# Values' three split terms as two stacked products and four bands, in the wide attentions of a four-layer transformer kernel

## The chip, the cores and the metric

The kernel runs on one core of one Trainium2 chip. The metric is the device time of a whole launch in microseconds: the median of the runs. The core has five engines with queues of their own that meet only through semaphores: TensorE (PE; its weight loads are the rows PEld), VectorE (DVE), ScalarE (ACT), GpSimd (POOL) and SyncE (SP), which here issues all transfers.

## The reference, cut to what matters

`x` is 128 x 64 tokens of width 128; `ctx_768`, the context, is 128 x 64 tokens of width 96. Four layers follow one another; each adds to `x` a cross attention of normalised `x` to the context and then a feed-forward part. All is float32.

```python
# layer: heads, width of a head      L0: 8, 128   L1: 16, 8   L2: 16, 64   L3: 16, 64
x = x + xattn(layernorm(x), ctx_768, Wq, Wk, Wv, Wo, bo)   # softmax over the 64 context tokens of a sequence
x = x + ffn(layernorm(x), ...)
```

L0, L2 and L3 are the "wide" attentions that the change touches; L1 is the "narrow" one. With M = Wv Wo of a head (96 x 128), the kernel forms a head's values as context times M, so that no output projection is left.

## The kernel before, in words

**Tiles.** The 8192 tokens are 64 tiles of 128, handled in 16 groups of 4 tiles (`NG`, `G`). `wide_attention` takes 4 heads per step: Q = 2 steps per group in L0 (`paired` is false, 32 steps), Q = 4 in L2 and L3 (`paired`, 64 steps each). That is 160 steps.

**Split products.** These matmuls take operands in a rounded format (`F32R`). For float32 accuracy each factor is split into a rounded high part and the rest, and `product` (L285 to L291) adds three matmuls of 512 columns: high x high (L288), low x high (L290), high x low (L291). For values the stationary side is 128 context tokens of `ct_hi` or `ct_lo` (96 rows) and the moving side `M_hi` or `M_lo` for 4 heads (96 x 512). So a step has 4 values products (V0 to V3, one per tile), 12 matmuls with 96 of the array's 128 rows used.

**A step on TensorE** (`group` on `block.tensor`): projections P0 and P1 (L288 to L291), transposes of the probabilities of the step two back (L577), P2, P3, V0, V1, V2, V3, then `output` (L598, 64 small matmuls for the step two back) and `scores` (L617, in L0 L620, 64 small ones). In the last step of a group the next group's tokens are transposed too (L237). P, T and V fills take turns in four PSUM banks (`Rotation`): V0 and V1 take the banks of the transposes, V2 and V3 those of P2 and P3, the next step's P0 and P1 those of V0 and V1. So V3 waits until ScalarE has kept P3 (`P_kept`), and P0 of the next step until V0 was copied out.

**The others in a step.** ScalarE, in this order: keep P0, P1 (L708), T0 (L718), exponentials of the step before (L723), T1, P2, P3, then values V0 and V2 (L713). VectorE: maxima and subtraction of the scores of the step before (L810, L813), extra work at fixed steps (normalising the next group, L220, at k = Q-2; `finish`, L837 and L305 to L313, at k = 2, in L0 at k = 0; in L0 the `quantise` steps of the first groups), totals and reciprocal (L818, L821), values V1 and V3 (L825), and at the group's end the split of the tokens (L254, L256). GpSimd: multiplication of the probabilities by the reciprocals (L511), and at k = 1 of each group from the second on `split_context` for the next group: high part (L389), then, behind a semaphore, the rest (L392). TensorE waits for it (`ct_split`) before P0 of the next group's first step.

**Start of a wide attention.** TensorE forms M for all heads (L541; in L0 also the folded query-key matrices, L539). ScalarE rounds it (`keep_folded`, L690), VectorE takes the rest (`keep_rest`, L786): 2 rounds in L0, 4 in L2 and L3. In L2 and L3 VectorE then does the token scales, for which ScalarE takes a square root (`scales.root`, L330) ahead of its first copy of P0; in L0 TensorE waits for all rests before it transposes the first tokens (L237).

**SyncE** loads the context of group j (96 x 512 floats, L377, L383) once the scores of group j-2 are done.

Of the kernel before, what the change touches and what calls it, by code (L numbers as in the profile page):

```python
# [14 lines left out]
F32 = mybir.dt.float32  # L15
# [392 lines left out]
def wide_attention(c, tag, heads, dh, scale):  # L408
# [3 lines left out]

    nc, dram = c.nc, c.dram
# [3 lines left out]
    with ExitStack() as st:  # L417
# [4 lines left out]
        M_hi, M_lo = (sb(f"M{n}{tag}", [K, heads, D], F32R) for n in ("_hi", "_lo"))  # L422
# [18 lines left out]
        fold_bank = (c.bank[1], c.bank[2], c.bank[3], c.bank[7]) if paired else (c.bank[1], c.bank[3])  # L441
# [3 lines left out]
        folded, hi_kept, lo_kept = sem("folded"), sem("hi_kept"), sem("lo_kept")  # L445
# [29 lines left out]
        with nc.Block() as block:  # L475
            @block.sync
            def _(sp):
# [10 lines left out]
                first_contexts(sp, c, "ctxP", ct, ct_in)  # L488
# [10 lines left out]
                later_contexts(sp, c, "ctxP", ct, ct_in, S_done, Q, 0)  # L499

            @block.gpsimd
            def _(pool):
# [3 lines left out]
                for j in range(2):  # L506
                    split_context(nc, pool, c, ct, ct_hi, ct_lo, j, j, 0, ct_in, ct_split)
# [6 lines left out]
                def group(i, slot, turn=None):  # L514
                    for k in range(Q):
                        if k or started(i, 1):
                            multiply(i * Q + k - 1, (slot * Q + k - 1) % 2)
                        if k == 1 and turn is not None:
                            split_context(nc, pool, c, ct, ct_hi, ct_lo, i + 1, 1 - slot, turn, ct_in, ct_split)
# [9 lines left out]
            def _(pe):  # L529
# [16 lines left out]
                else:  # L546
                    pe.wait_ge(lo_kept, 2 * rounds)
# [3 lines left out]
                def projection(m, i, slot, k, u, step):  # L551
                    x_parts = c.xT_hi[slot][:, :], c.xT_lo[slot][:, :]
                    ct_parts = ct_hi[slot][:, :], ct_lo[slot][:, :]
# [11 lines left out]
                def value(m, slot, k, u, step):  # L565

                    tok = slice(u * P, (u + 1) * P)
# [38 lines left out]
                def scores(m, i, slot, k):  # L606
                    for p in range(2):
                        for t in range(4):
                            for b in range(2):
                                for h in range(2):  # L610
# [8 lines left out]
                                    else:  # L619
                                        last = nc.tensor.matmul(out, proj[:, 2 * h + p, tok], ct[slot][:, ctx],  # L620
# [3 lines left out]
                def group(i, slot):  # L624
                    for k in range(Q):
# [24 lines left out]
                        if m == 0 and paired:  # L650
                            pe.wait_ge(lo_kept, 6)
# [14 lines left out]
                for n in (NS - 2, NS - 1):  # L666
# [9 lines left out]
                    output(n, n // Q, n % Q, n % 4)  # L676
# [3 lines left out]
            def _(act):  # L680
# [3 lines left out]
                def keep_folded(r):  # L684
# [5 lines left out]
                    nc.scalar.activation(M_hi[:, hs, :], fold_bank[r][0:K, :].rearrange("p (h d) -> p h d", h=4),  # L690
# [20 lines left out]
                def keep_value(m, u, step):  # L711
                    act.wait_ge(V_done, 4 * m + u + 1)
                    nc.scalar.activation(values[:, step % 4, u, :, :].rearrange("p h d -> p (h d)"),  # L713
# [47 lines left out]
            def _(dve):  # L761
# [37 lines left out]
                if paired:  # L799
                    keep_rest(2)  # L800
                    keep_rest(3)
# [21 lines left out]
                def keep_value(m, u, step):  # L823
                    dve.wait_ge(V_done, 4 * m + u + 1)
                    nc.vector.tensor_copy(values[:, step % 4, u, :, :].rearrange("p h d -> p (h d)"),  # L825
# [1753 lines left out]
```

## Time and profile before

| | us |
|---|---|
| median of 3 runs | 3574.77 (3566.44 to 3576.28) |
| profiled execution, its own time | 3565.56 |
| its span, first to last instruction | 3563.7 |
| TensorE, VectorE, ScalarE, GpSimd busy | 3440.1, 2463.3, 2024.0, 1244.5 |
| mean granted TensorE clock | 0.986 of full speed |

The profiled execution is 9.2 us below the median. Wide attentions lie at 0 to 394 us (L0), 1437 to 2071 (L2) and 2329 to 2963 (L3). In the timeline a row stands at its start, with its duration behind it; matmul durations overlap, so that their rate is read from the distance of the starts. "x2" means two in a row merged. What stands in brackets is the idle time of the engine before the row and who ended it.

### The profile page before, as it was taken

Reading aid. Unit: us, or ns where it says so; the run is one execution under the profiler, and the core shown is the slowest. Engines: PE = TensorE matmul, PEld = TensorE weight load, DVE = VectorE, ACT = ScalarE, POOL = GpSimd, SP = SyncE. Lnnn points to the kernel's source line nnn. Section 1 sums busy time; section 2 is a strip of 40 time slices with the busy share of each in tenths; the row PEclk is TensorE's granted clock in tenths of the full one; section 3 lists DMA queues with packets and bytes.
Section 4 is the critical chain, followed back from the end, with each engine's and each line's share of the span. In section 5 each row is a group of like instructions: output and inputs, shape, how many; then the busy total and the mean of one; then the engine's idle time right before and its main releaser. Section 6 shows DMA issues by size and latency. Waiting matters only on the chain. (4 is left out here: it accounts for less than half of the span.)

```text
span 3563.7 us, 99704 instructions
## 1 busy us (share of the span) xinstructions
PE 3440.1 (97%) x43493; PEld 2809.3 (79%) x43493; DVE 2463.3 (69%) x4927; ACT 2024.0 (57%) x3446; POOL 1244.5 (35%) x924
## 2 busy tenths in 40 slices
PE   7999999999999899999999999999999998999999
PEld 6887788887888555788888877778888886777777
DVE  8977555555666799666666656766666666777776
ACT  4445555554666787555555544455555555656564
POOL 1322233334554233222222223322222224555555
PEclk9999999999999899999999999999999999999999
DMA  3000000001000000000000000010000000000000
GB/s 110 11 11 11 1 1 1 1 1 38 15 15 9 1 1 1 18 9 7 7 9 7 5 22 1 1 47 9 7 7 9 7 5 1 7 7 13 7 7 13
DMA packets 15324, 40.66 MB, mean 11 GB/s; under 512 B 3083, under 2 KB 4683, under 8 KB 13994
## 3 DMA queue, kind: packets, MB, share of 16 engines
q1 hardware_dynamic: 14890, 34.28, 3.1%
q8 instruction: 345, 5.65, 0.7%
q14 instruction: 89, 0.73, 0.1%
HBM read 30.08 MB, written 4.19 MB: 10 GB/s over the span
## 5 line engine op out<-in xcount | busy, mean ns | idle before, releaser
L708 ACT ACTIVATE projL<-bank 128x512 f32<-128x512 f32 (+1 forms) x640 | 371.2, 601 | 647.3 <-PE bank L291 632.0
L511 POOL TENSOR_TENSOR probL<-probL,invL 128x1024 f32<-128x1024 f32 x160 | 304.7, 1904 | 1198.9 <-DVE invL L821 1198.9
L1704 POOL TENSOR_TENSOR h_loM<-hM,h_hiM 126x512 fp32r<-126x512 f32 x224 | 290.3, 1296 | 255.0 <-ACT h_hiM L1830 252.3
L598 PEld LDWEIGHTS bank<-valuesL,probTL 64*64 64x64 f32 x10240 | 277.7, 133 | 61.1 <-issue 55.2
L810 DVE TENSOR_REDUCE neg_maxL<-bank 128x16 f32<-128x1024 f32 x160 | 195.9, 1224 | 184.3 <-PE bank L617 153.4
L598 PE MATMUL bank<-valuesL,probTL 64*64 64x128 f32 x10240 | 316.4, 272 | 4.4 <-ACT probTL L718 4.4
L1403 PEld LDWEIGHTS bank<-w2T,hM 128*128 128x128 f32 x2304 | 278.4, 193 | 38.3 <-ACT hM L1458 22.9
L1403 PE MATMUL bank<-w2T,hM 128*128 128x128 f32 x2304 | 284.9, 277 | 15.4 <-ACT hM L1458 15.4
L1458 ACT ACTIVATE hM<-bank,ahead_scales 128x512 f32<-128x512 f32 x288 | 183.8, 684 | 189.3 <-PE bank L291 189.1
L825 DVE COPY valuesL<-bank 128x512 f32<-128x512 f32 x320 | 213.1, 679 | 109.5 <-PE bank L291 104.0
L818 DVE TENSOR_REDUCE totalL<-probL 128x16 f32<-128x1024 f32 x160 | 194.7, 1217 | 122.4 <-ACT probL L723 122.1
L1381 POOL TENSOR_TENSOR accM<-accM,partM 128x512 f32<-128x512 f32 x128 | 165.0, 1289 | 295.4 <-DVE partM L1488 295.4
L1942 DVE TENSOR_TENSOR tM<-bank,siluM 126x512 f32<-126x512 f32 x224 | 154.1, 688 | 115.9 <-PE bank L291 65.0
L713 ACT ACTIVATE valuesL<-bank 128x512 f32<-128x512 f32 x320 | 195.3, 611 | 56.4 <-PE bank L291 55.8
L1830 ACT ACTIVATE h_hiM<-hM 126x512 fp32r<-126x512 f32 x224 | 140.6, 628 | 133.1 <-DVE hM L1966 132.1
L718 ACT ACTIVATE probTL<-bank 128x512 f32<-128x512 f32 x320 | 188.3, 591 | 25.0 <-PE bank L577 25.0
L813 DVE TENSOR_TENSOR probL<-bank,neg_maxL 128x1024 f32<-128x1024 f32 x160 | 195.9, 1224 | 5.5
L1824 ACT ACTIVATE siluM<-bank 126x512 f32<-126x512 f32 x224 | 132.0, 590 | 97.1 <-PE bank L291 95.3
L1488 DVE TENSOR_TENSOR partM<-bank,gatesM 128x512 f32<-128x512 f32 x128 | 88.4, 690 | 128.4 <-PE bank L1403 127.2
L723 ACT ACTIVATE probL<-probL 128x1024 f32<-128x1024 f32 x160 | 169.3, 1058 | 2.9 <-DVE probL L813 2.8
L577 PEld LDWEIGHTS bank<-ident,probL 128*128 128x128 f32 x1280 | 149.9, 141 | 24.0 <-POOL probL L511 1.8
L577 PE MATMUL bank<-ident,probL 128*128 128x128 f32 x1280 | 167.2, 273 | 0.5 <-POOL probL L511 0.4
(300 smaller groups left out, 9033.3 us busy)
## 6 DMA issues: line engine op xcount, KB each, us to landing
ct0L<-in_ctxP SPq DMA_DIRECT2D x24, 192.0 KB, 2.4
ct1L<-in_ctxP SPq DMA_DIRECT2D x24, 192.0 KB, 2.5
x<-in_x SPq DMA_DIRECT2D x4, 1024.0 KB, 10.8
out<-x SPq DMA_DIRECT2D x8, 512.0 KB, 2.6
nct<-in_ctxP SPq DMA_DIRECT2D x16, 192.0 KB, 2.4
ahead_second<-in_L0w SPq DMA_DIRECT2D x2, 1152.0 KB, 17.9
ahead_second<-in_L3gate SPq DMA_DIRECT2D x1, 882.0 KB
ahead_second<-in_L3up SPq DMA_DIRECT2D x1, 882.0 KB
```

The costliest lines, as they stand in the source:

```text
L511: nc.gpsimd.tensor_tensor(segments(prob[:, slot, :]), segments(prob[:, slot, :]), per_segment(inv[:, slot, :]), ALU.mult).then_inc(prob_re ...
L577: last = nc.tensor.transpose(rot.bank(step, f"T{half}")[:, u * P:(u + 1) * P], prob[:, prob_slot, cols], c.ident[:, :])
L598: last = nc.tensor.matmul(o_bank[b * SEQ:(b + 1) * SEQ, t, u * D:(u + 1) * D], probT[t * SEQ:(t + 1) * SEQ, 2 * s + u, b * SEQ:(b + 1) * SEQ],
L708: nc.scalar.activation(proj[:, u, :], rot.bank(step, f"P{u}")[0:rows, :], ACT.Copy, scale=scale if paired and u % 2 == 0 else 1.0).then_in ...
L713: nc.scalar.activation(values[:, step % 4, u, :, :].rearrange("p h d -> p (h d)"), rot.bank(step, f"V{u}")[:, :], ACT.Copy).then_inc(Veven ...
L718: nc.scalar.activation(probT[:, 4 * half:4 * half + 4, :].rearrange("p s q -> p (s q)"), rot.bank(step, f"T{half}")[:, :], ACT.Copy).then_ ...
L810: nc.vector.tensor_reduce(neg_max[:, prob_slot, :], segments(s_bank.rearrange("p h c -> p (h c)")), axis=AX.X, op=ALU.max, negate=True).th ...
L813: nc.vector.tensor_tensor(segments(prob[:, prob_slot, :]), segments(s_bank.rearrange("p h c -> p (h c)")), per_segment(neg_max[:, prob_slo ...
L818: nc.vector.tensor_reduce(total[:, prob_slot, :], segments(prob[:, prob_slot, :]), axis=AX.X, op=ALU.add).then_inc(total_ready, 1)
L825: nc.vector.tensor_copy(values[:, step % 4, u, :, :].rearrange("p h d -> p (h d)"), rot.bank(step, f"V{u}")[:, :]).then_inc(Vodd_kept, 1)
L1403: last = nc.tensor.matmul(y_bank[ex % NY][:, t * D:(t + 1) * D], h[:, (n + j) % NH, t * P:(t + 1) * P], W2[:, 2 * ex + j, :], start=(t == ...
L1704: nc.gpsimd.tensor_tensor(h_lo[:, a % SLOTS, :], h[:, a % 3, :], h_hi[:, a % SLOTS, :].bitcast(F32), ALU.subtract).then_inc(lo_ready, 1)
```

## The change

In the wide attentions the three terms of a values product, 3 x 96 = 288 rows of contraction, are laid out as 128 + 128 + 32 rows. T1 (stationary) holds the high part of context rows 0 to 95 and, in rows 96 to 127, the low part of rows 0 to 31; T2 the high part of rows 0 to 63 and the low part of rows 32 to 95; T3 the high part of rows 64 to 95, for each of the 4 tiles in its own band of 32 partitions. M1, M2 and M3 are their partners. A step's values are now 8 matmuls of 128 rows and, at the end, 4 of 32 rows, each in a band of its own and into its own bank (`values_rest`). Only these signal `V_done`. The context comes in as three tensors (A and B 128 x 512, C 128 x 128). GpSimd forms T1 to T3 in 5 operations, in L2 and L3 6, since their key projections still need `ct_lo`. `keep_rest` has 8 VectorE operations per round; in L2 and L3 rounds 2 and 3 move into steps 1 and 2 of the first group. `values` has three slots instead of four, and step m uses slot m mod 3.

```diff
@@ buffers of wide_attention @@
-        M_hi, M_lo = (sb(f"M{n}{tag}", [K, heads, D], F32R) for n in ("_hi", "_lo"))
+        M1, M2, M3 = (sb(f"M{n}{tag}", [P, heads, D], F32R) for n in (1, 2, 3))
-        ct = [sb(f"ct{s}{tag}", [K, GT]) for s in range(2)]
-        ct_hi, ct_lo = ([sb(f"ct{n}{s}{tag}", [K, GT], F32R) for s in range(2)] for n in ("_hi", "_lo"))
+        raw = [[sb(f"ct{n}{s}{tag}", [P, cols]) for n, cols in (("A", GT), ("B", GT), ("C", P))] for s in range(2)]
+        T1, T2 = ([sb(f"T{n}{s}{tag}", [P, GT], F32R) for s in range(2)] for n in (1, 2))
+        T3 = [sb(f"T3{s}{tag}", [P, P], F32R) for s in range(2)]
+        ct_lo = [sb(f"ct_lo{s}{tag}", [K, GT], F32R) for s in range(2)] if paired else None
-        values = sb(f"values{tag}", [P, 4, 4, 4, D])
+        values = sb(f"values{tag}", [P, 3, 4, 4, D])
-        fold_bank = (c.bank[1], c.bank[2], c.bank[3], c.bank[7]) if paired else (c.bank[1], c.bank[3])
+        fold_bank = c.bank[0:4] if paired else (c.bank[1], c.bank[3])
+        parts = 6 if paired else 5
@@ SyncE @@
+                def load_context(j):
+                    for dst, name in zip(raw[j % 2], ("ctxA", "ctxB", "ctxC")):
+                        cols = dst.shape[1]
+                        sp.dma_start(dst[:, :], dram[name][:, j * cols:(j + 1) * cols]).then_inc(ct_in[j % 2], 16)
@@ GpSimd, in place of split_context @@
+                def stack_context(j, slot):
+                    A, B, C = raw[slot]
+                    pool.wait_ge(ct_in[slot], 48 * (j // 2 + 1))
+                    for part, high in ((A, T1[slot]), (B, T2[slot]), (C, T3[slot])):
+                        nc.gpsimd.tensor_tensor(high[:, :], part[:, :], c.one[:, :].to_broadcast([P, part.shape[1]]), ALU.mult)\
+                            .then_inc(ct_split, 1)
+                    pool.wait_ge(ct_split, parts * j + 3)
+                    if paired:
+                        nc.gpsimd.tensor_tensor(ct_lo[slot][:, :], A[0:K, :], T1[slot][0:K, :].bitcast(F32), ALU.subtract)\
+                            .then_inc(ct_split, 1)
+                    for n, (part, high, rows) in enumerate(((A, T1[slot], slice(96, P)), (B, T2[slot], slice(64, P)))):
+                        pool.wait_ge(ct_split, parts * (j + 1) - 2 + n)
+                        nc.gpsimd.tensor_tensor(high[rows, :], part[rows, :], high[rows, :].bitcast(F32), ALU.subtract)\
+                            .then_inc(ct_split, 1)
+                    pool.wait_ge(ct_split, parts * (j + 1))
@@ TensorE @@
                 def value(m, slot, k, u, step):
-                    weights = tuple(M[:, 4 * k:4 * k + 4, :].rearrange("p h d -> p (h d)") for M in (M_hi, M_lo))
-                    product(nc, rot.bank(step, f"V{u}")[:, :], (ct_hi[slot][:, tok], ct_lo[slot][:, tok]), weights)\
-                        .then_inc(V_done, 1)
+                    for n, (tokens, weights) in enumerate(((T1, M1), (T2, M2))):
+                        nc.tensor.matmul(rot.bank(step, f"V{u}")[:, :], tokens[slot][:, tok],
+                                         weights[:, heads_of, :].rearrange("p h d -> p (h d)"), start=(n == 0), stop=False,
+                                         skip_group_check=True)
+
+                def values_rest(slot, k, step):
+                    for u in range(4):
+                        band = slice(32 * u, 32 * u + 32)
+                        nc.tensor.matmul(rot.bank(step, f"V{u}")[:, :], T3[slot][band, :],
+                                         M3[band, 4 * k:4 * k + 4, :].rearrange("p h d -> p (h d)"), start=False, stop=True,
+                                         skip_group_check=True).then_inc(V_done, 1)
...
-                            pe.wait_ge(ct_split, 2 * i + 2)
+                            pe.wait_ge(ct_split, parts * (i + 1))
...
-                        if m == 0 and paired:
-                            pe.wait_ge(lo_kept, 6)
+                        if paired and i == 0:
+                            pe.wait_ge(stack_kept, max(2, k + 1) if k < 2 else 4)
...
                         value(m, slot, k, 3, step)
+                        values_rest(slot, k, step)
                         if older:
-                            output(n, back[0], back[1], bstep % 4)
+                            output(n, back[0], back[1], n % 3)
@@ ScalarE and VectorE @@
-                    nc.scalar.activation(M_hi[:, hs, :], fold_bank[r][0:K, :].rearrange("p (h d) -> p h d", h=4),
+                    nc.scalar.activation(M1[0:K, hs, :], fold_bank[r][0:K, :].rearrange("p (h d) -> p h d", h=4),
                                          ACT.Copy).then_inc(hi_kept, 1)
...
                     dve.wait_ge(hi_kept, r + 3 if paired else 2 * r + 2)
-                    nc.vector.tensor_tensor(M_lo[:, hs, :].rearrange("p h d -> p (h d)"), fold_bank[r][0:K, :],
-                                            M_hi[:, hs, :].bitcast(F32).rearrange("p h d -> p (h d)"), ALU.subtract)\
-                        .then_inc(lo_kept, 1)
+                    for M, to, rows in ((M1, slice(96, P), slice(0, 32)), (M2, slice(64, 96), slice(32, 64)),
+                                        (M2, slice(96, P), slice(64, 96))):
+                        nc.vector.tensor_copy(flat(M, to), fold_bank[r][rows, :])
+                    nc.vector.tensor_tensor(flat(M2, slice(0, 64)), fold_bank[r][0:64, :],
+                                            flat(M1, slice(0, 64)).bitcast(F32), ALU.subtract)
+                    for u in range(4):
+                        last = nc.vector.tensor_tensor(flat(M3, slice(32 * u, 32 * u + 32)), fold_bank[r][64:96, :],
+                                                       flat(M1, slice(64, 96)).bitcast(F32), ALU.subtract)
+                    last.then_inc(stack_kept, 1)
...
                 keep_rest(0)
                 keep_rest(1)
                 if paired:
-                    keep_rest(2)
-                    keep_rest(3)
...
                         if k or started(i, 1):
                             maxima(m - 1, (step - 1) % 2)
+                        if paired and i == 0 and k in (1, 2):
+                            keep_rest(k + 1)
@@ lay_out @@
+    o["ctxA"] = np.concatenate([o["ctxP"], o["ctxP"][0:32]])
+    o["ctxB"] = np.concatenate([o["ctxP"][0:64], o["ctxP"][32:96]])
+    o["ctxC"] = o["ctxP"][64:96].reshape(32, NG, 4, P).transpose(2, 0, 1, 3).reshape(P, NG * P)
```

## Rows read from the trace of the kernel before

**Rows 1.** The page: busy time, share of the span, instructions, by engine.

```profile
PE 3440.1 (97%) x43493; PEld 2809.3 (79%) x43493; DVE 2463.3 (69%) x4927; ACT 2024.0 (57%) x3446; POOL 1244.5 (35%) x924
```

**Rows 2.** Windows: length, busy us of PE, PEld, DVE, ACT, POOL, clock; L2.

```profile
1443.00:2071.00 628.00, 624.87 (x10338) 528.05 (x10336) 416.81 (x708) 345.98 (x599) 155.31 (x94) 0.99 0.02 7
```

**Rows 3.** Timeline, one step of L2: start, us, engine, line, operation, tiles.

```profile
1605.41 0.50 PE L288 MATMUL bank<-xT_hi,wq_hiL 128*128 128x512 f32 x1
...
1609.17 0.39 PE L288 MATMUL bank<-M_hiL,ct_hi0L 96*128 96x512 f32 x1
1609.40 0.39 PE L290 MATMUL bank<-M_hiL,ct_lo0L 96*128 96x512 f32 x1
...
1612.01 1.98 PE L598 MATMUL bank<-valuesL,probTL 64*64 64x128 f32 x64
...
1614.85 0.50 PE L288 MATMUL bank<-xT_hi,wq_hiL 128*128 128x512 f32 x1
```

**Rows 4.** Groups by line and shape: count, busy us, mean ns, idle before.

```profile
L617 PE MATMUL bank<-projL 64*64 64x64 f32 x8192 | 142.4, 218 | 0.0
...
L620 PE MATMUL bank<-ct0L,projL 96*64 96x64 f32 x1024 | 34.1, 224 | 0.0
```

**Rows 5.** Timeline: ScalarE's copies of P2 and P3; a TensorE wait on such.

```profile
1609.50 1.09 ACT L708 ACTIVATE projL<-bank 128x512 f32<-128x512 f32 x2
...
1459.11 0.50 PE L288 MATMUL bank<-M_hiL,ct_hi0L 96*128 96x512 f32 x1 [0.39 <-ACT projL L708]
...
1459.45 0.40 PE L290 MATMUL bank<-M_hiL,ct_lo0L 96*128 96x512 f32 x1
```

**Rows 6.** Timeline, one group of L0, from its start to the next group's.

```profile
201.47 0.47 PE L288 MATMUL bank<-xT_hi,A_hiL 128*96 128x512 f32 x1
...
212.17 1.23 DVE L810 TENSOR_REDUCE neg_maxL<-bank 128x16 f32<-128x1024 f32 x1 [2.41 <-PE bank L620]
...
219.23 1.04 POOL L389 TENSOR_TENSOR ct_hi1L<-ct1L,one 96x512 fp32r<-96x512 f32 x1
...
220.35 1.33 POOL L392 TENSOR_TENSOR ct_lo1L<-ct1L,ct_hi1L 96x512 fp32r<-96x512 f32 x1
...
223.02 0.47 PE L288 MATMUL bank<-xT_hi,A_hiL 128*96 128x512 f32 x1
```

**Rows 7.** An earlier group end of L0; then TensorE's waits (us, times, longest), 0-400.

```profile
134.77 1.60 POOL L392 TENSOR_TENSOR ct_lo1L<-ct1L,ct_hi1L 96x512 fp32r<-96x512 f32 x1
...
136.47 0.45 PE L288 MATMUL bank<-xT_hi,A_hiL 128*96 128x512 f32 x1 [0.62 <-issue]
...
PE bank L288 <- issue: 4.3, 4, 2.3
```

**Rows 8.** Timeline, the start of L2, to the fourth step.

```profile
1440.27 0.69 DVE L786 TENSOR_TENSOR M_loL<-bank,M_hiL 96x512 fp32r<-96x512 f32 x1
...
1445.13 0.18 DVE L346 TENSOR_SCALAR var_eps<-stats 128x64 f32<-128x64 f32 x1
...
1446.69 0.77 PE L288 MATMUL bank<-xT_hi,wq_hiL 128*128 128x512 f32 x1
...
1449.39 0.63 PE L288 MATMUL bank<-M_hiL,ct_hi0L 96*128 96x512 f32 x1
...
1454.06 1.22 DVE L810 TENSOR_REDUCE neg_maxL<-bank 128x16 f32<-128x1024 f32 x1 [0.43 <-PE bank L617]
...
1471.27 0.50 PE L288 MATMUL bank<-xT_hi,wq_hiL 128*128 128x512 f32 x1
```

**Rows 9.** Timeline, the start of L0.

```profile
19.54 0.66 PE L237 MATMUL bank<-ident,xh 128*128 128x128 f32 x4 [2.23 <-DVE M_loL L786]
```

**Rows 10.** Timeline: VectorE's copies in L2, and L220 without and with GpSimd busy.

```profile
1621.95 1.22 DVE L825 COPY valuesL<-bank 128x512 f32<-128x512 f32 x2
...
1617.38 1.11 DVE L220 TENSOR_SCALAR xh<-x,stats,rstd 128x128 f32<-128x128 f32 x4
...
15.30 2.06 DVE L220 TENSOR_SCALAR xh<-x,stats,rstd 128x128 f32<-128x128 f32 x4
```

More of the change, by code:

```diff
@@ L498, in _ @@
                     c.ahead.load_experts(sp)
-                later_contexts(sp, c, "ctxP", ct, ct_in, S_done, Q, 0)
+                for j in range(2, NG):
+                    sp.wait_ge(S_done, (j - 1) * Q)
+                    load_context(j)
             @block.gpsimd
@@ L505, in _ @@
                     pool.wait_ge(one_set, 1)
-                for j in range(2):
-                    split_context(nc, pool, c, ct, ct_hi, ct_lo, j, j, 0, ct_in, ct_split)
+                def stack_context(j, slot):
[13 more added lines that the diff above has]
+                    pool.wait_ge(ct_split, parts * (j + 1))
+                stack_context(0, 0)
+                stack_context(1, 1)
                 def multiply(n, slot):
@@ L518, in group @@
                         if k == 1 and turn is not None:
-                            split_context(nc, pool, c, ct, ct_hi, ct_lo, i + 1, 1 - slot, turn, ct_in, ct_split)
+                            stack_context(i + 1, 1 - slot)
                 group(0, 0)
@@ L546, in _ @@
                 else:
-                    pe.wait_ge(lo_kept, 2 * rounds)
+                    pe.wait_ge(lo_kept, rounds)
+                    pe.wait_ge(stack_kept, rounds)
                     pe.wait_ge(ident_in, 16)
@@ L552, in projection @@
                     x_parts = c.xT_hi[slot][:, :], c.xT_lo[slot][:, :]
-                    ct_parts = ct_hi[slot][:, :], ct_lo[slot][:, :]
+                    ct_parts = (T1[slot][0:K, :], ct_lo[slot][:, :]) if paired else None
                     out = rot.bank(step, f"P{u}")[0:rows, :]
@@ L619, in scores @@
                                     else:
-                                        last = nc.tensor.matmul(out, proj[:, 2 * h + p, tok], ct[slot][:, ctx],
+                                        last = nc.tensor.matmul(out, proj[:, 2 * h + p, tok], raw[slot][0][0:K, ctx],
                                                                 start=True, stop=True)
@@ L675, in _ @@
                     wait_for_output(n, n // Q, n % Q)
-                    output(n, n // Q, n % Q, n % 4)
+                    output(n, n // Q, n % Q, n % 3)
                 keep_warm(nc, c, rot.bank(NS + 1, "T0"), 15)
@@ L712, in keep_value @@
                     act.wait_ge(V_done, 4 * m + u + 1)
-                    nc.scalar.activation(values[:, step % 4, u, :, :].rearrange("p h d -> p (h d)"),
+                    nc.scalar.activation(values[:, m % 3, u, :, :].rearrange("p h d -> p (h d)"),
                                          rot.bank(step, f"V{u}")[:, :], ACT.Copy).then_inc(Veven_kept, 1)
@@ L785, in keep_rest, with flat @@
                     dve.wait_ge(hi_kept, r + 3 if paired else 2 * r + 2)
-                    nc.vector.tensor_tensor(M_lo[:, hs, :].rearrange("p h d -> p (h d)"), fold_bank[r][0:K, :],
-                                            M_hi[:, hs, :].bitcast(F32).rearrange("p h d -> p (h d)"), ALU.subtract)\
-                        .then_inc(lo_kept, 1)
+                    def flat(M, rows):
+                        return M[rows, hs, :].rearrange("p h d -> p (h d)")
+                    for M, to, rows in ((M1, slice(96, P), slice(0, 32)), (M2, slice(64, 96), slice(32, 64)),
[7 more added lines that the diff above has]
+                    last.then_inc(stack_kept, 1)
                 if paired:
@@ L824, in keep_value @@
                     dve.wait_ge(V_done, 4 * m + u + 1)
-                    nc.vector.tensor_copy(values[:, step % 4, u, :, :].rearrange("p h d -> p (h d)"),
+                    nc.vector.tensor_copy(values[:, m % 3, u, :, :].rearrange("p h d -> p (h d)"),
                                           rot.bank(step, f"V{u}")[:, :]).then_inc(Vodd_kept, 1)
```

6 lines of the change are left out of this document (4 added, 2 removed).

## The prediction

> **What bounds the kernel now.** I read the page's busy line first: TensorE is busy for 3440 of 3564 us, VectorE for 69% [rows 1]. The windows by stage say whether that holds where the change is: in L2, 624.9 of 628 us at 0.99 of the full clock [rows 2]; L3 reads alike, and in L0 TensorE has small gaps. So here its instruction stream is the time, and what shortens the stream counts, as long as nobody is late for it. A timeline of one step shows the stream: P0 at 1605.41, V0 at 1609.17, `output` at 1612.01, the next P0 at 1614.85, a step of 9.44 us, with a 512-column matmul every 0.23 us [rows 3]. The values part, V0 to `output`, takes 2.84 us: 12 x 0.23 and 0.1 for the change to 64-row tiles.
>
> **Part 1: the values matmuls.** Eight of 128 rows replace eight of the twelve at the same 0.23 us, as projections with 128 rows run no slower: 1.87 us. What the four bands cost no row shows. If they ran one after the other they would take 0.94, together 0.23. The nearest rows: 64x64 score matmuls cost 142.4 us / 8192 = 17.4 ns each, those of 96 rows, which cannot share the rows of the array, 34.1 / 1024 = 33.3 ns [rows 4]. Two row groups thus give 1.9-fold; four at 1.9 squared give 0.94 / 3.6 = 0.26, and I take 0.30, since four 128-column weights load behind a change of tile shape. A second such change costs 0.1 as the first. Sum: 1.87 + 0.1 + 0.30 + 0.1 = 2.37, a gain of 0.47 us per step, from 0.54 (bands 0.23) to a loss of 0.17 (bands in series).
>
> The Trainium skill gives a figure for this very packing (TensorE: Matmul & The Clock Gate, Measured speedup vs the span model): four tiles of 32 rows and 512 columns run 3.07 times as fast. By it the bands would be 0.94 / 3.07 = 0.305, an estimate; no run here shows it yet.
>
> **Part 2: what is late next.** V3 needs P3's bank, so it waits for ScalarE's copy of P3. That ends at 1609.50 + 1.09 = 1610.59, 1.42 after V0's start [rows 3, 5]. Before, V3 started 9 x 0.23 = 2.10 after V0, with 0.7 to spare; now 6 x 0.23 = 1.40, and 1.42 with some 0.07 of semaphore is 1.49. A matmul behind such a wait also has its successor 0.34 rather than 0.23 behind it (1459.11, 1459.45) [rows 5]. The copy hangs on the exponentials and the maxima of the scores, so it does not move. This takes 0.09 to 0.20 of the 0.47; I keep 0.32 per step, and 0.27 to 0.47 as its range where bands overlap.
>
> All copies of values now start behind the bands. ScalarE's two take 1.2 us and VectorE's two 1.22 [rows 10], within the 2.84 of `output` and `scores` [rows 3]: no cost for most steps. At k = 2 of L2 and L3 it is closer: VectorE's copies ended at 1621.95 + 1.22 = 1623.17, the scores one step behind 1614.85, at 1624.3. GpSimd's work for the context grows (part 3) and now lies beside VectorE's normalising. Four L220 took 2.06 us with GpSimd busy and 1.11 without [rows 10], so VectorE loses 0.95 and, with L837, some 1.2 us. It is then late for the scores by 0.3 us, once per group: 30 x 0.3 = 9 us, from 0 to 18. The three slots of `values` cost nothing: slot m mod 3 was read by `output` in the step before on the same queue. Three transfers for one (576 KB for 192) lie far ahead of their use.
>
> **Part 3: GpSimd in L0.** `split_context` was 1.04 + 0.08 + 1.33 us. Added are B's high part (1.04), C's (0.3, a quarter of the columns), one more rest (1.33; fewer partitions with the same 512 columns, no row shows it shorter) and a semaphore gap of 0.08: 2.8 us, bounds 1.5 and 3.2. In L2 and L3 one more, 1.3 us, but with Q = 4 there are two and a half steps of cover. In L0 there is almost none, because the context is made in the last step of the group and TensorE waits for it before the next P0. The timeline: group start 201.47, scores of k = 0 done at 212.1, GpSimd done at 220.35 + 1.33 = 221.68, next group at 223.02 [rows 6]. The cover is 1.34 us. GpSimd's chain starts with the scores of k = 0, which come 0.47 earlier. So the next group starts 2.8 - 0.47 - 1.34 = 1.0 us later, not earlier. In four group ends GpSimd was already last, as VectorE had quantising to do: it ended at 136.37 and P0 began at 136.47 after an idle 0.62; four such waits sum to 4.3 us [rows 7]. There the loss is 2.33. Fourteen ends: 4 x 2.33 + 10 x 1.0 = 19.3 us. Gains of the four steps outside, -1.6.
>
> **Part 4: the starts.** `keep_rest` has eight 512-column operations for one. In rows two like copies out of a bank follow at 0.53 us (1.22 for two [rows 10]), and one alone is 0.69 (L786). The new ones read one set of partitions and write another; no row shows such neighbours, so I take the slow end, 8 x 0.69 = 5.5 per round, with 8 x 0.53 = 4.3 as the other.
>
> On this the Trainium skill has a rule (VectorE: DVE Perf Modes, Two Vector instructions with no wait between them): an instruction whose input or output starts in another group of 32 partitions than its forerunner's is held until all earlier ones have finished. All eight would be held, which gives 5.5; without the rule 4.3. No row of the trace decides between them.
>
> L0: two rounds were 2 x 0.69 of the queue that TensorE waited 2.23 us for [rows 9]; now 11. Transposes and all behind move by about +10 us.
> L2, L3: the rests of rounds 0 and 1 run from 1440.27 to 1451.3, then the scales (before at 1445.13): +6.2. ScalarE sits in the square root ahead of its copy of P0, and P2 at 1446.69 needs that copy: TensorE moves by +6.2 [rows 8]. Then rounds 2 and 3 on VectorE. From the first scores (t = 0 at 1454.06): maxima to 2.45, round 2 to 8.0, totals and copies to 10.6, maxima of step 1 to 13.1, round 3 to 18.6. V0 of step 2 waits for it (`stack_kept` 4), and its scores end at 18.7 + 2.4 + 2.9 = 24.0, against 1471.27 - 1454.06 = 17.2 before: +6.7. With 0.3 saved before that and 1.5 for matmuls at 1.2 GHz behind the idle times (0.63 recorded rather than 0.39, as at 1449.39 [rows 3, 8]) it is +14 per layer, from 9 to 16, with the three steps' own gains in it.
>
> **Sum**, against the profiled execution (3565.6): L0 start +10.0, L0 group ends +19.3, its other steps -1.6, L2 and L3 starts +28, their lateness at k = 2 +9, 2 x 61 steps x -0.32 = -39.0. Together +25.7. The median stands 9.2 above the profiled execution; on it I get 3574.8 + 25.7 = 3600.5, and say 3600.
>
> **Rivals.**
> 1. Bands beside each other and beneath the full-size matmuls, no wait in V3 (the faster one). Place: each step's values part. Nine matmul times and one change of shape, 2.20 us, would gain 0.64 a step: 122 x 0.64 = 78 for 39, so -13 and 3561. For: the queue already loads weights under running matmuls. Against: 0.1 at each change of shape, and the copy of P3. It turns faster above 0.32 + 25.7 / 122 = 0.53 a step, and beyond the measurable at 0.62. Chance 0.12.
> 2. VectorE's rests overlap at 0.53: L0's start 2.5 less, L2's and L3's 5.1 each: +13, 3588; with no lateness at k = 2 either +4, 3579. For: all come out of banks, whose copies overlap in rows 10. Chance 0.20.
> 3. The bands do not overlap: each step takes 0.17 + 0.1 more than before, and the sum is 25.7 + 39 + 33 = +98, 3672. Against: [rows 4]. Chance 0.06.
> 4. GpSimd's time goes with its partitions, so that the 32- and 64-row rests take 0.5 and 0.9: 1.3 less per end, -14 to -18, 3584. Chance 0.07.
>
> The forecast has 0.55: 3583 to 3622. A measurement of this kernel tells 0.3%, 10.7 us, from no change. Slower: the forecast, rival 3, most of 4 and half of 2, 0.72. Same: 0.16, faster: 0.12. The range 3570 to 3640 leaves out rival 3 and most of rival 1, with one side's tail of the forecast.
>
> **What would show it.** In the profile after: a V0-to-`output` distance of 2.4 to 2.6 us in L2 (part 1), with V3 waiting for L708 (part 2); four bands within 0.3 us. In L0 TensorE idle before the first matmul of each group, behind GpSimd, and a group of 22.6 us for 21.55 (part 3). Eight VectorE operations 0.7 apart in each round, TensorE idle for some 6 us behind P1 of L2's and L3's first step and some 5 before V0 of the third (part 4). The prediction is wrong if L0's groups are not longer, or if L2's steady step falls below 8.9 us.

## The result: slower by 2.0%

The changed kernel takes 3641.22 us (median of 4 runs, 3634.16 to 3654.91), the kernel before 3575.1 on the same chip (4 runs, 3566.44 to 3576.28): a ratio of 1.020, with an interval of 1.0176 to 1.0223. The forecast was 3600, in a range of 3570 to 3640: slower, as most of its chance had it, but 41 us too little and just outside its range. The profiled execution took 3641.05 us, its span 3639.2, 75.5 more than before; the mean granted clock fell from 0.986 to 0.973.

The page of the changed kernel, busy time by engine, answers to [rows 1]:

```profile
PE 3437.4 (94%) x43493; PEld 2713.6 (75%) x43493; DVE 2544.3 (70%) x4997; ACT 2031.6 (56%) x3446; POOL 1421.2 (39%) x1100
```

TensorE's instructions are as many as before (eight and four for the twelve) and its busy time is the same, while the span grew by 75: the loss is waiting, and time at half clock. GpSimd has 176 instructions and 177 us more, VectorE 70 and 81.

The blocks of score matmuls, of which each step has one, divide the 75.5 us:

| stretch | before | after | difference |
|---|---|---|---|
| start to L0's first scores | 30.1 | 42.9 | +12.8 |
| L0's other 31 steps | 344.3 | 386.3 | +42.0 |
| L0's last scores to L2's start | 1062.4 | 1070.6 | +8.2 |
| L2's start to its third scores | 33.4 | 50.6 | +17.2 |
| L2's other 61 steps | 585.2 | 575.6 | -9.6 |
| L2's last scores to L3's third | 306.6 | 322.3 | +15.7 |
| L3's other 61 steps, and its end | 1201.7 | 1190.9 | -10.8 |

Nothing in the third stretch was changed. Its 8.2 us lie in L1's attention, where the granted clock was 0.79 over 40 us (second row; before it was 1.00 there). The stretch of L1's output matmuls measured 290.3 us before, 298.1 after, and between 290.8 and 310.5 in the ten profiles of the experiments, all with the same code there. So at least most of it is a spread of single executions; that the one profile of before lies at its lower end leaves a part open. Windows of the changed kernel (length, busy PE, PEld, DVE, ACT, POOL, clock, DMA share, GB/s), L0's steps first:

```profile
60.00:430.00 370.00, 326.99 (x4809) 253.26 (x4807) 268.09 (x548) 170.36 (x291) 134.75 (x100) 0.95 0.07 23
1065.00:1105.00 40.00, 39.46 (x1006) 34.18 (x997) 21.84 (x41) 22.50 (x37) 18.18 (x17) 0.79 0.05 13
```

The same for L0 of the kernel before, up to its last scores. TensorE was busy for 308.0 of 315 us at full clock; after, for 327.0 of 370 at 0.95:

```profile
60.00:375.00 315.00, 308.01 (x4630) 253.19 (x4630) 260.26 (x502) 162.52 (x280) 89.59 (x57) 1.00 0.04 10
```

What TensorE waits for in that stretch of the changed kernel (us, times, longest); before it was 4.3 us in four times [rows 7]:

```profile
PE bank L288 <- issue: 38.5, 14, 5.4
```

One group end of L0, in the timeline of the changed kernel, answers to [rows 6]:

```profile
230.59 1.90 POOL L541 TENSOR_TENSOR probL<-probL,invL 128x1024 f32<-128x1024 f32 x1 [8.04 <-DVE invL L869]
232.45 1.04 POOL L524 TENSOR_TENSOR T10L<-ctA0L,one 128x512 fp32r<-128x512 f32 x1
233.45 1.28 POOL L524 TENSOR_TENSOR T20L<-ctB0L,one 128x512 fp32r<-128x512 f32 x1
233.87 1.41 DVE L256 TENSOR_TENSOR xT_lo<-xT,xT_hi 128x512 fp32r<-128x512 f32 x1
234.69 0.84 POOL L524 TENSOR_TENSOR T30L<-ctC0L,one 128x128 fp32r<-128x128 f32 x1
235.68 1.26 POOL L532 TENSOR_TENSOR T10L<-ctA0L,T10L 32x512 fp32r<-32x512 f32 x1
237.02 1.26 POOL L532 TENSOR_TENSOR T20L<-ctB0L,T20L 64x512 fp32r<-64x512 f32 x1
238.38 0.54 PE L288 MATMUL bank<-xT_hi,A_hiL 128*96 128x512 f32 x1 [2.27 <-issue]
238.72 0.63 PE L290 MATMUL bank<-xT_hi,A_loL 128*96 128x512 f32 x1
239.15 0.63 PE L291 MATMUL bank<-xT_lo,A_hiL 128*96 128x512 f32 x1
```

The reader is to see three things. The next group's P0 starts 0.1 us behind GpSimd's last rest, 238.28, so that is what "issue" hides. GpSimd's two high parts beside VectorE's split of x (L254, L256) took 1.28 and 0.84 rather than the 1.04 and 0.40 that they take alone. And behind the wait the matmuls start 0.43 us apart rather than 0.23: half clock, from 238.6 to 242.0. Not every wait has such a stretch. Of the 14, the four longest (3.4 to 5.5 us) have one beside them, and of the ten of 2.3 us four have one and six have none.

A later group of the same kernel, all of it at full clock, shows the lateness alone: start of the group, first and last operation on the context, start of the next group.

```profile
335.25 0.45 PE L288 MATMUL bank<-xT_hi,A_hiL 128*96 128x512 f32 x1 [2.25 <-issue]
...
352.85 1.04 POOL L524 TENSOR_TENSOR T11L<-ctA1L,one 128x512 fp32r<-128x512 f32 x1
...
357.42 1.26 POOL L532 TENSOR_TENSOR T21L<-ctB1L,T21L 64x512 fp32r<-64x512 f32 x1
358.78 0.44 PE L288 MATMUL bank<-xT_hi,A_hiL 128*96 128x512 f32 x1 [2.27 <-issue]
```

It takes 23.53 us, before 21.55 [rows 6], so 2.0 more without any half clock.

In L2, one step's values part answers to [rows 3]; with it stand the two of ScalarE's copies on which V1 (1640.97) and V3 (1642.03) wait:

```profile
1640.33 0.58 ACT L758 ACTIVATE probTL<-bank 128x512 f32<-128x512 f32 x1
1640.47 0.40 PE L600 MATMUL bank<-M1L,T11L 128*128 128x512 f32 x1
1640.70 0.40 PE L600 MATMUL bank<-M2L,T21L 128*128 128x512 f32 x1
1640.81 1.08 ACT L748 ACTIVATE projL<-bank 128x512 f32<-128x512 f32 x2
1640.97 0.50 PE L600 MATMUL bank<-M1L,T11L 128*128 128x512 f32 x1
1641.30 0.40 PE L600 MATMUL bank<-M2L,T21L 128*128 128x512 f32 x1
...
1641.79 0.40 PE L600 MATMUL bank<-M2L,T21L 128*128 128x512 f32 x1
1642.03 0.44 PE L600 MATMUL bank<-M1L,T11L 128*128 128x512 f32 x1
1642.31 0.40 PE L600 MATMUL bank<-M2L,T21L 128*128 128x512 f32 x1
1642.63 0.50 PE L607 MATMUL bank<-M3L,T31L 32*128 32x512 f32 x4
1643.06 1.98 PE L637 MATMUL bank<-valuesL,probTL 64*64 64x128 f32 x64
```

V0 to `output` takes 2.59 us in this step (k = 0) and at k = 1, before 2.84 to 2.87. Steps, from P0 to P0, as medians over L2:

| k | before | after | V0 to `output`, after |
|---|---|---|---|
| 0 | 9.48 | 9.20 | 2.59 |
| 1 | 9.44 | 9.20 | 2.59 |
| 2 | 9.48 | 9.35 | 2.74 |
| 3 | 9.88 | 9.87 | 2.80 |

A group of four steps takes 37.62 us, before 38.27.

The start of L2, VectorE and then TensorE, answers to [rows 8]:

```profile
1503.77 0.68 DVE L832 CAST M1L<-bank 32x512 fp32r<-32x512 f32 x1 [0.54 <-ACT M1L L730]
1504.46 1.39 DVE L832 CAST M2L<-bank 32x512 fp32r<-32x512 f32 x2
1505.87 0.68 DVE L833 TENSOR_TENSOR M2L<-bank,M1L 64x512 fp32r<-64x512 f32 x1
1506.56 2.79 DVE L836 TENSOR_TENSOR M3L<-bank,M1L 32x512 fp32r<-32x512 f32 x4
1509.38 0.68 DVE L832 CAST M1L<-bank 32x512 fp32r<-32x512 f32 x1
...
1512.19 0.77 PE L288 MATMUL bank<-xT_hi,wq_hiL 128*128 128x512 f32 x1 [3.97 <-POOL T20L L532]
1516.72 0.77 PE L288 MATMUL bank<-xT_hi,wq_hiL 128*128 128x512 f32 x1 [1.63 <-ACT projL L748]
```

Eight operations take 5.6 us, one every 0.69 to 0.70. TensorE then first waits for GpSimd's context, and then for ScalarE, which sits in the root behind VectorE's rests.

### The profile page after: what moved, and what is told of

Read it like the earlier page. It is cut to its first block and busy times, and to the rows that moved or that the text cites. A ratio compares the mean times of both kernels' runs of the same rounds, so it can differ in the third digit from the quotient of the medians.

```text
span 3639.2 us, 100117 instructions
## 1 busy us (share of the span) xinstructions
PE 3437.4 (94%) x43493; PEld 2713.6 (75%) x43493; DVE 2544.3 (70%) x4997; ACT 2031.6 (56%) x3446; POOL 1421.2 (39%) x1100
## 5 line engine op out<-in xcount | busy, mean ns | idle before, releaser
L1754 POOL TENSOR_TENSOR h_loM<-hM,h_hiM 126x512 fp32r<-126x512 f32 x224 | 290.8, 1298 | 253.8 <-ACT h_hiM L1880 251.1
L873 DVE COPY valuesL<-bank 128x512 f32<-128x512 f32 x320 | 203.9, 679 | 181.0 <-PE bank L607 180.9
L753 ACT ACTIVATE valuesL<-bank 128x512 f32<-128x512 f32 x320 | 173.9, 596 | 226.2 <-PE bank L607 226.2
## 6 DMA issues: line engine op xcount, KB each, us to landing
x<-in_x SPq DMA_DIRECT2D x4, 1024.0 KB, 10.9
```

The lines of the kernel that those rows point to most:

```text
L873: nc.vector.tensor_copy(values[:, m % 3, u, :, :].rearrange("p h d -> p (h d)"), rot.bank(step, f"V{u}")[:, :]).then_inc(Vodd_kept, 1)
L1754: nc.gpsimd.tensor_tensor(h_lo[:, a % SLOTS, :], h[:, a % 3, :], h_hi[:, a % SLOTS, :].bitcast(F32), ALU.subtract).then_inc(lo_ready, 1)
```

## The experiments

All ratios are to the kernel before on the same chips, with 95% intervals. Theory A, with which I went in: L0's group ends are what the forecast had too small, because GpSimd stacks the context behind its last multiply of the group, TensorE waits for it with no cover, and each wait is followed by a stretch at half clock (the rows above show that for eight of 14). Its rivals: the loss sits in L2 and L3; or it sits in the starts, where VectorE keeps the rests.

**Which layer.** `wide_attention_before` is the function as it was before the change; `e1` uses it for L0, `e2` for L2 and L3.

```
- (narrow_attention if layer == "L1" else wide_attention)(...)
+ (narrow_attention if layer == "L1" else wide_attention_before if layer == "L0" else wide_attention)(...)   # e1
+ (narrow_attention if layer == "L1" else wide_attention_before if layer != "L0" else wide_attention)(...)   # e2
```

> L0 keeps the wide attention of before; L2 and L3 have the changed one. My theory: L0 carries most of the loss (54.8 us between the last scores of L0 before and after), L2 and L3 some 7.5 each, 8 us lie in a stretch of half clock in L1 that has nothing to do with the change. So +15 us, a ratio of 1.004, and TensorE idle before P0 only in the four group ends of before. Rival (a cost that all three attentions share, such as the threefold context loads or the bands' own price): two thirds of the loss would stay, since L2 and L3 have 128 of 160 steps: +45 us, 1.012.

> Only L0 has the changed wide attention; L2 and L3 that of before. My theory: +50 to +55 us, a ratio of 1.014 to 1.0155, in one fifth of the steps. Rival (shared cost): +10 to +20 us. The sum of this run's and the other part's loss should be that of the whole change, 66 us, if the layers are independent.

Measured: `e1` 3584.35 us, 1.0052 (1.0023 to 1.0081); `e2` 3627.36 us, 1.0171 (1.0139 to 1.0202). The two losses add up to 0.0223 for the whole's 0.020. L0 alone has three quarters or more; L2 and L3 together still lose 0.5%, since their starts cost more than 122 steps give.

**What in L0: the order on GpSimd.** The context of the next group is stacked one step earlier, ahead of that step's wait for the maxima and totals. All its work stays.

```
- if k == 1 and turn is not None:
+ if k == (1 if paired else 0) and turn is not None:
      stack_context(i + 1, 1 - slot)
```

> The changed kernel, but in L0 GpSimd makes the next group's stacked context in the first step of a group instead of the second, some 10 us earlier; no work is left out. Theory (in L0 TensorE waits at each group end for GpSimd, 39 us of idle, and runs behind each wait at 1.2 GHz for some microseconds): the idle before P0 goes, L0's clock is 1.0 from group to group, a group takes 20.8 to 21.2 us instead of 24.3, and the kernel 45 us less: 3596, ratio 1.006. Rival (GpSimd's and VectorE's collisions on memory, which the longer context work brings wherever it stands, set the group): less than 15 us comes back, 3626 or more.

Measured: 3590.49 us, 1.0065 (1.0043 to 1.0087). L0's last scores came at 383.3 rather than 429.2, 45.9 us sooner, and its groups, from the fourth on, took 21.2 to 22.6 us rather than 23.5 to 26.6. GpSimd's rows with the context early, and the window:

```profile
221.72 1.04 POOL L524 TENSOR_TENSOR T11L<-ctA1L,one 128x512 fp32r<-128x512 f32 x1
...
223.71 0.40 POOL L524 TENSOR_TENSOR T31L<-ctC1L,one 128x128 fp32r<-128x128 f32 x1
...
225.61 1.29 POOL L532 TENSOR_TENSOR T21L<-ctB1L,T21L 64x512 fp32r<-64x512 f32 x1
228.44 1.91 POOL L541 TENSOR_TENSOR probL<-probL,invL 128x1024 f32<-128x1024 f32 x1 [1.53 <-DVE invL L869]
```

```profile
60.00:380.00 320.00, 311.48 (x4711) 238.86 (x4709) 256.98 (x538) 168.64 (x289) 131.12 (x100) 1.00 0.09 26
```

The same five instructions end 1.5 us ahead of the next multiply's input and cost TensorE nothing; the clock is at 1.00, the wait named "issue" is gone from the list. The place, and not the work, was the price. L0's 31 steps take 341.2 us now, before the change 344.3.

**The half-clock share of it.** Eight matmuls into a bank that P0 overwrites fill a part of each wait, so that TensorE is busy while it waits; their result is not used.

```
  if k == 0:
+     if not paired and i:
+         pe.wait_ge(Veven_kept, 2 * m + 1)
+         for _ in range(8):
+             nc.tensor.matmul(rot.bank(step, "P0")[:, :], M1[:, 0, :], M1[:, 0:4, :]..., start=True, stop=True)
      pe.wait_ge(xT_split, 2 * i + 2)
      pe.wait_ge(ct_split, parts * (i + 1))
```

> The changed kernel with eight matmuls of 512 columns, whose result nobody reads, issued on TensorE at each group start of L0 before it waits for GpSimd: the wait stays, the array does not idle. This parts the wait from the clock. Theory (of L0's 42 us behind its start some 20 are matmuls at half clock behind the waits): L0's groups go from 24.3 to 22.6 to 23.2 us, the kernel gets 15 to 25 us faster than the changed one, 3616 to 3626, ratio 1.012 to 1.014, with the granted clock of L0 near 1.0. Rival (the wait alone): no gain, or a loss of up to 5 us where the filler outlasts the wait, ratio 1.018 or more.

Measured: 3620.29 us, 1.0149 (1.0125 to 1.0173); L0's last scores came 12.8 us sooner, with work added.

```profile
60.00:410.00 350.00, 335.54 (x4804) 255.93 (x4803) 263.22 (x541) 163.77 (x283) 133.29 (x99) 1.00 0.08 24
```

The clock stands at 1.00 and GpSimd's lateness remains: each group still starts 0.10 us behind its last rest, and eight of them take 23.5 to 23.6 us, for the 22.6 to 23.2 expected. L0's 31 steps take 373.7 us, for 386.3 in the changed kernel and 344.3 before. So of the 42.0 us that they lost 12.6 were half clock, and 29.4 the lateness itself.

**Moving the exponentials.** If V1 and V3 wait for ScalarE's copies of T1 and P3, the exponentials, which sit ahead of both, are in their way. They go behind the copies.

```
- if k or started(i, 1):
-     exponentials(m - 1, (step - 1) % 2)
  ...
  keep_projection(m, 3, step)
+ if k or started(i, 1):
+     exponentials(m - 1, (step - 1) % 2)
```

> The changed kernel with ScalarE's exponentials behind its copies of T1, P2 and P3 instead of between T0 and T1. In the changed kernel's trace ScalarE runs T0, exponentials, T1, P2, P3 without a gap, and V1 waits for T1's copy, V3 for P3's: the values part of L2 takes 2.59 us at k = 0 and 1, 2.83 at k = 2, 2.73 at k = 3. Theory (these waits hold back the gain of the bands): it becomes 2.4 at each k, a group of L2 and L3 36.5 to 36.8 us instead of 37.6, the kernel 25 to 35 us faster than the changed one: about 3610, ratio 1.009 to 1.012. Rival (the exponentials' own chain over VectorE and GpSimd to the transposes has no 2 us to give): the transposes wait instead and nothing is gained, ratio 1.018 to 1.022.

Measured: 3749.07 us, 1.0482 (1.0434 to 1.0531), worse than either expectation. V0 to `output` became 2.37 us at each k, as the theory had it, and in L2 the steps k = 0 to 2 took 8.98 us; but k = 3 took 14.1, and a group 41.0. L0's groups took 27.3. What TensorE waits for, over the whole span of this kernel:

```profile
PE bank L288 <- issue: 68.7, 15, 6.1
PE bank L288 <- DVE xT_lo L256: 36.9, 32, 3.4
PE bank L288 <- DVE valuesL L873: 36.4, 30, 2.9
PE bank L616 <- POOL probL L541: 20.3, 33, 0.7
```

The exponentials feed totals, reciprocals, GpSimd's multiply and only behind that the context. Later by one copy, each of these is late, and VectorE's own copies of values stand behind its totals.

**Context early everywhere.** The same edit as in `e3`, for L2 and L3 too: `if k == 0`.

> GpSimd makes the next group's context in the first step of each group in all three wide attentions, also in L2 and L3 (there at k = 0 instead of 1). In L2's step k = 2 the four L220 took 2.57 us beside GpSimd's work against 1.11 before, and VectorE's copies of the values came late. Theory (this collision costs L2 and L3 0.2 to 0.4 us per group): beside the gain in L0 (3590 in the run with L0 alone moved) another 5 to 12 us, ratio 1.003 to 1.005. Rival (VectorE's lateness at k = 2 is covered, the step is held by ScalarE alone): the same as with L0 alone, 1.0065, within 0.002.

Measured: 3588.39 us, 1.0042 (1.0017 to 1.0067); against `e3`'s 1.0065 the intervals overlap, so the times alone don't settle it. The trace shows the group of L2 at 37.44 us for 37.62, 0.18 less, some 5 us over both layers. It takes GpSimd from beside VectorE's L220 at k = 2, which took 2.57 us there in the changed kernel and 1.11 here. All of the 0.18 is in the step behind it, k = 3 (9.69 for 9.87); k = 2 itself stays at 9.35 (below).

**The spacing of VectorE's rests.** Rounds 0 and 1 of L2 and L3 are interleaved, so that each operation has a neighbour with the same partitions.

```
  for M, to, rows in ((M1, slice(96, P), slice(0, 32)), ...):
+     for r in range(2):
          nc.vector.tensor_copy(flat(M, to, r), fold_bank[r][rows, :])
```

> One look at VectorE's spacing. In L2 and L3 the sixteen operations of the rests of rounds 0 and 1 are issued in pairs: the same source and target partitions for round 0 and then for round 1. In the changed kernel all are 0.69 to 0.70 us apart. Theory (an operation whose source or target starts in another group of 32 partitions than its forerunner's is held until that one has ended): inside a pair the distance falls to 0.53 us, between pairs it stays at 0.69, and the sixteen take 9.8 instead of 11.2 us. Rival (operations on few partitions, or out of a bank with rounding, always take 0.69): all distances stay. The time of the kernel is not to be told from the changed one's: 2 to 3 us.

A single run, 3637.02 us. VectorE's rows:

```profile
1502.34 1.28 DVE L849 CAST M1L<-bank 32x512 fp32r<-32x512 f32 x2 [2.61 <-ACT M1L L730]
1503.63 2.59 DVE L849 CAST M2L<-bank 32x512 fp32r<-32x512 f32 x4
1506.24 1.28 DVE L851 TENSOR_TENSOR M2L<-bank,M1L 64x512 fp32r<-64x512 f32 x2
1507.54 5.21 DVE L855 TENSOR_TENSOR M3L<-bank,M1L 32x512 fp32r<-32x512 f32 x8
```

Sixteen operations take 10.4 us for 11.2: a pair takes 1.28 to 1.30, so its second starts 0.59 to 0.60 behind its first, and 0.69 follow. The neighbours' partitions do set the spacing, but the 0.53 of the copies in [rows 10] was not reached. Why it was not is open. From a single run the time can't be told from the changed kernel's.

**The starts.** L0's transposes no longer wait for the rests of the values' weights; those rests follow the first split of x, round 1 one step later. In L2 and L3 the first part of the scales goes ahead of the rests.

```
- pe.wait_ge(stack_kept, rounds)          # L0, ahead of its transposes
+ if not paired and i == 0:               # ahead of the first V0s
+     pe.wait_ge(stack_kept, k + 1)
  ...
+ scale_steps.pop(0)()                    # L2, L3: ahead of the rests
```

> The changed kernel with other starts, no work left out: in L2 and L3 VectorE gives ScalarE the variances first, so that the square root does not hold back the copy of P0; in L0 the first tokens are transposed and split before the rests of M, and round 1 moves into step 1. Theory (the starts cost 12.8 us in L0 and 17 in each of L2 and L3, of which the root's wait is 1.8 a layer, the rest being VectorE's 5.6 us per round): L0's first scores end 6 to 9 us earlier, L2's and L3's by 1.5 to 2, but in L0 VectorE is busy with statistics in the first steps and takes part of it back. 6 to 12 us in all, ratio 1.016 to 1.018. Rival (GpSimd's first context, done 12 us into L2, sets the start): nothing in L2 and L3, only L0's 3 to 8.

Measured: 3631.69 us, 1.0154 (1.0105 to 1.0202). The interval overlaps that of the changed kernel, 1.0176 to 1.0223, so a gain is not shown by the times. L0's first scores come at 32.0, 10.9 us sooner, but its second, at 48.5, only 3.7 sooner and its last 5.4. What VectorE now does in between, the rest of round 1 ahead of the statistics of x, is the likely reason; no run parts it. In L2 the third scores follow the first by 26.8 us instead of 27.4. The starts are a debt that this order mostly moves.

**Everything together.** `e9` joins `e6`, `e5` and `e8`; with the context early, the chain in which `e5` lost has slack. `e10` is `e9` with the exponentials last only where it pays in L2 and L3:

```
+ late = not paired or k < 2
- if k or started(i, 1):
+ if (k or started(i, 1)) and not late:
      exponentials(m - 1, (step - 1) % 2)
  ...
  keep_projection(m, 3, step)
+ if (k or started(i, 1)) and late:
+     exponentials(m - 1, (step - 1) % 2)
```

> The stacked values with all repairs together: context made in the first step of a group in all wide attentions, exponentials behind P3's copy, the other starts. Theory: the terms are in different places and add. Early context -45 to -55, exponentials -25 to -35 in L2 and L3 and, with L0 no longer waiting for GpSimd, another -5 to -10 there, starts -6 to -12, from 3641: 3535 to 3560, faster than the kernel before by 0.3 to 1%. Rival (VectorE becomes the bound as the step shrinks, above all at k = 2 and in L0's groups): 3565 to 3590, no faster than before.

> As the run with all repairs, but in L2 and L3 the exponentials stand behind P3's copy only at k = 0 and 1, and in their old place at k = 2 and 3, where VectorE has the token split to finish before the next group. In the run with all repairs the steps of L2 took 8.97, 8.99, 9.42 and 10.08 us, with TensorE waiting 1.1 us for the split tokens at each group end; with the early exponentials 9.20, 9.20, 9.35 and 9.69. Theory (late exponentials gain 0.22 a step where VectorE has slack and lose at the group end where it has none): 8.97, 8.99, 9.35, 9.69, a group of 37.0 us for 37.47, 32 times 0.45, so 14 us less than the run with all repairs: 3552, ratio 0.995 to 0.997. Rival (the late chain of k = 1 already makes VectorE late through k = 2 and 3): 37.3 to 37.5 us a group and the same 3567.

Measured: `e9` 3566.70 us, 0.9994 (0.9980 to 1.0008), no difference to before, where 3535 to 3560 were expected; `e10` 3556.84 us, 0.9977 (0.9960 to 0.9994), faster than before by 0.2%. In `e9` the group of L2 takes 37.47 us, with steps, P0 to P0, of 8.97, 8.97, 8.99 and 10.53: V0 to `output` is 2.37 at every k, but at the end of k = 3 TensorE waits for the split of x. (The expectation of `e10` counts from scores to scores, which gives 8.97, 8.99, 9.42 and 10.08 with the same sum.) In `e10` the steps are 8.97, 8.99, 9.35 and 9.69, the group 37.00; L2's other 61 steps take 566.4 us for 585.2 before. L0's last scores come at 373.3, against 374.4 before. The wait of TensorE in L2, 1500 to 2060, in `e9`; the list of `e10` has no such row:

```profile
PE bank L288 <- DVE xT_lo L256: 15.6, 15, 1.1
```

## Why the prediction was right or wrong

**The step that failed is part 3's price of a group end in L0**: "2.8 - 0.47 - 1.34 = 1.0 us later", with the half clock behind the waits put at nothing. The mechanism and the place were right: TensorE idle before the group's first matmul, behind GpSimd, and `e3` shows that it is GpSimd's place in the order. But L0's 31 steps lost 42.0 us where the forecast had 17.7.

At full clock a group end cost 2.0 us and not 1.0. The group from 335.25 gives the terms. The context work took 5.83 us (352.85 to 358.68) for the 5.25 of the sum, since two of the high parts lie beside VectorE's split of x: 0.58 more. It began 17.60 us behind the group's start, before 17.76 [rows 6]; the forecast had it 0.47 earlier, and it was 0.16, because L0's scores of k = 0 came only 0.17 earlier (they end 10.27 us behind the group's start, before 10.44). That is 0.31 more. Part 3 had taken part 1's whole gain there, though part 2 kept only 0.32 of it. And P0 starts 0.10 behind GpSimd's end, which the sum had left out. Together 0.99. The waits of 2.3 us are longer than the 2.0, since TensorE, with shorter steps, also comes to them earlier. By `e4` the lateness cost 29.4 us over L0's steps, 11.7 more than forecast.

The other 12.6 us are half clock, by `e4` too. The forecast had charged it to the starts of L2 and L3, where the rows showed it, and not to these waits.

**Part 1 was right.** The eight matmuls start 0.23 to 0.33 apart, and the four bands take 0.43 us up to `output` with one change of shape in it, so 0.33 beside the 0.1; 0.30 was forecast, and in series it would have been 0.94. Where no copy is waited for, in `e5` and `e9`, V0 to `output` is 2.37 us, the forecast's sum. Rival 3 is out, and rival 1 too, as the changes of shape and the copies' waits are there. By the Trainium skill (TensorE: Matmul & The Clock Gate, Measured speedup vs the span model) four such tiles would take 0.305, an estimate; the trace agrees within 0.03.

**Part 2 was right in kind and half in size.** V3 waits for P3's copy. V1 waits for T1's copy as well, which I had missed: it starts 0.27 behind its forerunner, and its second matmul 0.33 behind that. A step of k = 0 or 1 gains 0.24 to 0.28, for the forecast's 0.32: the waits take 0.22 of the values part (2.59 for 2.37), and not 0.15. Steps of k = 2 gain 0.13 and of k = 3 0.01: in L2 61 steps gave 9.6 us and in L3 10.3, for 19.5 less 4.5 expected. For k = 3 one reason is plain, since the copy of x (L245) sits between those of P2 and P3 on ScalarE. Of the changed kernel, ScalarE:

```profile
1668.76 0.59 ACT L748 ACTIVATE projL<-bank 128x512 f32<-128x512 f32 x1
1669.23 0.60 ACT L245 ACTIVATE xT<-bank 128x512 f32<-128x512 f32 x1
1669.71 0.61 ACT L748 ACTIVATE projL<-bank 128x512 f32<-128x512 f32 x1
```

The forecast's lateness of 0.3 us per group, from VectorE's normalising beside GpSimd, was there, but one step on. L220 took 2.57 us, and in `e6`, in which it takes 1.11, P3's copy of the step k = 3 ends 1.47 us behind V0 rather than 1.63, and that step is 0.18 shorter.

At k = 2 P3's copy ends 1.42 behind V0, as at k = 0 and 1, but V3 starts 0.26 behind that end and not 0.13 (medians over L2; in the group below 1660.29 and 1660.63). TensorE's queue has one more condition ahead of V3 there, `out_read` of `wait_for_output`, which VectorE's addition of the output (L879) had met long before. The trace's records of TensorE's waiting instructions show that at k = 2 the one on P3's copy is followed by another, 0.11 to 0.20 us behind it, while at every other k the one on P3's copy is the last. That extra instruction is the likely cost; no run takes it out, so this is argued and not shown.

```profile
1657.64 2.57 DVE L220 TENSOR_SCALAR xh<-x,stats,rstd 128x128 f32<-128x128 f32 x4
...
1659.20 1.09 ACT L748 ACTIVATE projL<-bank 128x512 f32<-128x512 f32 x2
...
1660.19 0.40 PE L600 MATMUL bank<-M2L,T21L 128*128 128x512 f32 x1
...
1660.63 0.47 PE L600 MATMUL bank<-M1L,T11L 128*128 128x512 f32 x1
```

**Part 4 was near.** Rests come every 0.69 us, 5.6 per round, for 5.5; rival 2 is out. By the Trainium skill (VectorE: DVE Perf Modes, Two Vector instructions with no wait between them) an operation that starts in another group of 32 partitions than its forerunner is held until all earlier ones have finished. The trace agrees, and so does `e7`, in which equal partitions shortened the spacing. L0's start cost 12.8 us for 10, L2's 17.2 for 14. That of L2 has a wait that the forecast lacks: GpSimd's first context, 3.97 us of TensorE.

**Rival 4** (GpSimd's time by its partitions) is out: L532 has a median of 1.28 to 1.29 us on 32 rows and on 64 alike. The Trainium skill (GPSIMD Engine Reference, Architecture) says that each of GpSimd's cores owns 16 partitions. By that, fewer rows would leave cores idle and save no time; the rows agree.

The sum by terms, forecast and measured: L0's start 10 and 12.8, L0's steps 17.7 and 42.0, starts of L2 and L3 28 and 32.9, steps of L2 and L3 -30 and -19.9, L1 0 and 8.2, the ends of L3 0 and -0.5. Together 25.7 and 75.5. Of the 50 that are missing, 24 are the group ends (12 lateness, 13 half clock), 10 the small gain of the steps, 8 the two kinds of start, 8 L1's half clock, which another execution may not have. Between the medians the loss is 66 us; the profiled execution of before lay 9.2 below its median.

## What to carry to other kernels

Before a small cost is put on a second engine, look where in that engine's order it stands: 5.8 us of stacking cost TensorE some 46 us over the layer behind the last multiply of the group, and nothing one step earlier. Where a change makes TensorE wait some 2 us again and again, expect part of the matmuls behind the waits at half clock: here that was 12.6 us over 14 waits. When a gain is priced in one part of a forecast, use the same gain in the others. And a gain of 0.25 us in a stage is worth having only when its start debts are below what its steps give; here the starts cost 46 us and 122 steps of L2 and L3 gave 20.

## What the runs showed of the hardware

- Four matmuls of 32 rows and 512 columns in four bands, behind others of 128 rows, took 0.43 us with one change of shape, where a single one of 512 columns takes 0.23.
- Beside four of ten idle times of 2.3 us, and beside all four of 3.4 us and more, TensorE ran at 1.2 GHz for a while, with 0.63 us recorded for a matmul of 512 columns rather than 0.39; from 238.6 to 242.0 in the group shown. With matmuls in the idle times it stayed at 2.4 GHz (clock 1.00).
- GpSimd's subtraction of two inputs with 512 columns takes 1.28 to 1.29 us in the changed kernel (medians), whether it has 32, 64 or 96 rows.
- Beside VectorE's split of x, GpSimd's multiplications took 1.28 us with 512 columns and 0.84 with 128, alone 1.04 and 0.40.
- Beside GpSimd's stacking, VectorE's four normalising operations took 2.57 us for 1.11.
- VectorE's operations that read a bank and change partitions start 0.69 apart; with a neighbour in the same partitions 0.59 to 0.60.
